# Combining four experts on one Trainium2 core: seven more result tiles loaded while the softmax ends, gates in seven parts instead of six, and the carry of maxima moved ahead of the last block's sums

## The reference, cut to what matters

```python
def gnn(features, edge_src, edge_dst, edge_weight, W, b):        # 12500 nodes, 200000 edges, 256 features
    msgs = features[edge_src] * edge_weight[:, None]
    agg = segment_sum(msgs, edge_dst)
    return agg @ W.T + b

def ffn(x):                                                      # M = 8192: edge_index names nodes 0..8191
    h = (x @ W_gat).reshape(M, 4, 4)                             # heads, experts
    src, dst = edge_index with a loop at every node              # 131072 edges
    e = leaky_relu((h * att_src).sum(-1)[src] + (h * att_dst).sum(-1)[dst], 0.2)
    alpha = softmax of e over the edges of each dst
    agg = segment_sum(h[src] * alpha[:, :, None], dst) + b_gat
    scores = (layernorm(agg) * gamma + beta).mean over heads     # one score for each expert
    g = softmax over the two best scores, 0 for the other two
    for ei in range(4):
        out += g[ei] * (gelu(x @ W1[ei] + b1[ei]) @ W2[ei] + b2[ei])

x = x + gnn(layernorm(x));  x = x + ffn(layernorm(x))
```

## Time and the profile before

| | us |
|---|---|
| median of three runs | 3670.58 |
| the profiled execution | 3668.62 |
| its span in the profile | 3666.8 |
| last expert pair's sum by DVE ends | 3449.2 |
| last block of the softmax can begin | 3462.12 |
| first gather of `combine` | 3488.62 |
| PE's first pair in `combine` | 3518.51 |
| PE's last sum copied out | 3663.65 |

### The profile page before, as it was taken

One profiled execution on the slowest core, in us unless ns is written; L12 is line 12 of the kernel. 1 busy time (PEld: TensorE's weight loads), 2 busy tenths in 40 slices (PEclk: granted clock), 3 DMA queues, 4 the chain that ended last, 5 costly groups with the idle time before them and its releaser, 6 DMA issues. The chain is left out here.

```text
span 3666.8 us, 60445 instructions
## 1 busy us (share of the span) xinstructions
PE 2973.6 (81%) x13893; PEld 2432.7 (66%) x13894; DVE 2042.9 (56%) x6851; ACT 817.8 (22%) x2321; POOL 2708.2 (74%) x2817
## 2 busy tenths in 40 slices
PE   1475665666866889978888799999999999999648
PEld 1354544554645666766666688888888888888537
DVE  8777778787787676664344223343343334242567
ACT  6300000000111111211222222223232322232247
POOL 6677777777777777777777777777777777777573
PEclk6786887887877999999999899999999999999879
DMA  9643333333433444444444222242223222322289
GB/s 347 198 120 106 107 111 111 112 114 112 116 115 111 121 122 124 128 119 127 128 128 131 58 73 54 54 122 54 73 54 76 54 74 53 79 73 54 57 299 366
DMA packets 276554, 424.71 MB, mean 116 GB/s; under 512 B 59704, under 2 KB 210211, under 8 KB 275363
## 3 DMA queue, kind: packets, MB, share of 16 engines
q0 software_dynamic: 114208, 216.64, 23.6%
q1 hardware_dynamic: 64175, 114.71, 8.6%
q10 hardware_dynamic: 98004, 91.50, 7.7%
HBM read 317.12 MB, written 105.97 MB: 115 GB/s over the span
## 5 line engine op out<-in xcount | busy, mean ns | idle before, releaser
L672 POOL DMA_INDIRECT rows<-feats,src_t x1500 | 1446.8, 965 | 466.9 <-issue 443.6
L1198 POOL DMA_INDIRECT got<-row_dram,src_sorted x1024 | 990.0, 967 | 312.1 <-issue 312.1
L833 PE MATMUL node_sums<-rows,ys_ahead 128*128 x3904 | 989.5, 408 | 231.6 <-SPq L656 101.2
L833 PEld LDWEIGHTS node_sums<-rows,ys_ahead 128*128 128x128 f32 x3904 | 762.4, 202 | 427.5 <-issue 314.9
L1282 PE MATMUL d_hidden<-d_yt,w 128*128 128x256 f32 x3136 | 711.9, 380 | 0.8 <-DVE d_yt L1368 0.8
L1293 PE MATMUL d_expert<-w,hid 128*128 128x256 f32 x3136 | 708.7, 379 | 0.0
L1293 PEld LDWEIGHTS d_expert<-w,hid 128*128 128x128 f32 x3136 | 596.7, 190 | 80.2
L1282 PEld LDWEIGHTS d_hidden<-d_yt,w 128*128 128x128 f32 x3136 | 595.0, 191 | 79.7 <-DVE d_yt L1368 1.2
L1345 DVE TENSOR_TENSOR yo<-d_expert,x_and_b 128x512 f32<-128x512 f32 x196 | 135.5, 691 | 837.5 <-PE d_expert L1293 829.9
L892 DVE TENSOR_SCALAR ys_ahead<-iota,rel,ew_t 128x128 f32<-128x128 f32 x1952 | 557.1, 364 | 65.3 <-DVE rel L888 2.3
L1226 ACT ACTIVATE hid<-d_hidden,b1c 128x256 f32<-128x256 f32 x784 | 323.7, 471 | 983.8 <-PE d_hidden L1282 792.7
(11 more groups left out here) (302 smaller groups left out, 2270.2 us busy)
## 6 DMA issues: line engine op xcount, KB each, us to landing
y_dram<-yo ACTq DMA_DIRECT2D x196, 256.0 KB, 2.2
ys<-y_dram SPq DMA_DIRECT2D x36, 1024.0 KB, 9.2
rows<-feats,src_t POOLq DMA_INDIRECT x1500, 2.8
got<-row_dram,src_sorted POOLq DMA_INDIRECT x1024, 2.4
ys_ahead<-y_dram SPq DMA_DIRECT2D x13, 1024.0 KB, 9.1
x_dram<-edge_plan ACTq DMA_DIRECT2D x98, 128.0 KB
d_x<-x_dram ACTq DMA_DIRECT2D x49, 256.0 KB, 3.1
ys_ahead<-in_x ACTq DMA_DIRECT2D x97, 128.0 KB
```

What stands on the lines that cost most here:

```text
L672: pool.indirect_dma_start(rows[:, g % RING, j, :], None, feats, bass.IndirectOffsetOnAxis(ap=m.src_t[:, g * GT + j:g * GT + j + 1], axis=0 ...
L833: t = pe.matmul(psA[:, ds(((code >> 1) & 1) * 512, FEAT)], hot[:, r, j, :], rows[:, ds((code >> 2) & (RING - 1), 1), j, :], start=False, s ...
L1198: pool.indirect_dma_start(got[:, k, j, 0:ROWF], None, m.row_dram, bass.IndirectOffsetOnAxis(ap=m.src_sorted[:, BEGIN[b] + j:BEGIN[b] + j + ...
```

## The change

It has these parts.

- `AHEAD` becomes 5: the early load takes in pair 4, whose buffer is now part of the tile `m.plan`. `SLOTS` becomes 17.
- `LATE` = 7: after the store of the seventh block's states, and once PE, DVE and the stores are through with all pairs, SP loads pairs 5 to 11. Their buffers are the tiles of the expert weights `w1` and `w2` and the tiles `hid`, `yo` and `x_and_b2`, which live on to the end of the program for that. In `combine` SP first loads the three small vectors, then pairs 12 to 16.
- `PART` has seven parts of 6, 12, 18, 20, 18, 16 and 8 tiles instead of six of 10, 18, 20, 20, 20 and 10. DVE sums every third pair of a part instead of every fourth (18 pairs instead of 17, PE 31 instead of 32).
- In the last block of the softmax DVE's 4 and 20 scans are issued without a wait between them.
- `carry` is split. `carry_across` of the maxima (turn, copy, scan) stands right behind the last block's `maxima`; `carry_back` stands behind its `sums`.
- Nodes without edges get a place of their own behind the edges (128 rows of zeros in `state_dram`, written once by SP). The bounds checks of `spread` and of the gather go, and so does POOL's clearing of `m.ns`. `positions` on DVE has three more small instructions.

```diff
-SLOTS = 16
-AHEAD = 4
+SLOTS = 17
+AHEAD = 5
+LATE = 7
...
     pool.indirect_dma_start(m.adst_first, bass.IndirectOffsetOnAxis(ap=m.first_pos[:, t:t + 1], axis=0),
-                            m.node_dst[:, t, :], None, bounds_check=GEDGES - 1, oob_is_err=False
-                            ).then_inc(m.s_sc, 16)
+                            m.node_dst[:, t, :], None).then_inc(m.s_sc, 16)
...
                     for k in range(AHEAD):
-                        load_pair(sp, m, k, k, m.ys_ahead[:, k])
+                        load_pair(sp, m, k, k, m.y_slots[k])
+                if b == len(BLOCK_PAIR) - 1:
+                    sp.wait_ge(s_l2, PAIRS * EXPERTS)
+                    sp.wait_ge(s_yo, PAIRS * EXPERTS)
+                    for e in range(EXPERTS):
+                        sp.wait_ge(s_st[e], 16 * PAIRS)
+                    for k in range(AHEAD, AHEAD + LATE):
+                        load_pair(sp, m, k, k, m.y_slots[k])
...
-            pool.memset(m.ns, 0.0).then_inc(s_clear, 1)
...
                 for ch in range(start, stop):
-                    c.done(v.tensor_tensor_scan(rows[:, :, ch], decay[:, head[ch], 0:n], rows[:, :, ch],
-                                                last[:, ch:ch + 1], ALU.mult, ALU.add))
+                    c.inc(v.tensor_tensor_scan(rows[:, :, ch], decay[:, head[ch], 0:n], rows[:, :, ch],
+                                               last[:, ch:ch + 1], ALU.mult, ALU.add))
+                    if b < BLOCKS - 1 or ch == stop - 1:
+                        v.wait_ge(s_v, c.n)
...
-            for b in range(len(BLOCK_PAIR), BLOCKS):
-                maxima(b)
-                messages(b)
-                sums(b, 0, ROWF)
-                block_end(b)
-
-            c.inc(v.tensor_copy(tail[:, 0, 0:HEADS], mx[:, :, 0]))
+            maxima(BLOCKS - 1)
+            c.inc(v.tensor_copy(tail[:, 0, 0:HEADS], mx[:, :, size(BLOCKS - 1)]))
...
-            carry(0, HEADS, -BIG, ALU.min, ALU.max)
+            carry_across(0, HEADS, -BIG, ALU.min, ALU.max)
+            messages(BLOCKS - 1)
+            sums(BLOCKS - 1, 0, ROWF)
+            block_end(BLOCKS - 1)
+            carry_back(0, HEADS)
...
-        PART = [0, 10, 28, 48, 68, 88, T]
+        PART = [0, 6, 18, 36, 56, 74, 90, T]
         PARTS = len(PART) - 1
         BY_VECTOR = [i for n in range(PARTS) for i in range(PART[n] // 2, PART[n + 1] // 2)
-                     if (i - PART[n] // 2) % (4 if n < PARTS - 1 else 2) == 0]
+                     if (i - PART[n] // 2) % (3 if n < PARTS - 1 else 2) == 0]
...
-            for k in range(AHEAD, SLOTS // 2):
-                load_pair(sp, m, k, k, y_of(k))
             for n, a in enumerate((b_gat, gamma, beta)):
                 sp.dma_start(vec[:, n, :], a.rearrange("(o c) -> o c", o=1).to_broadcast([P, HE])).then_inc(s_c, 16)
-            for k in range(SLOTS // 2, SLOTS):
+            for k in range(AHEAD + LATE, SLOTS):
                 load_pair(sp, m, k, k, y_of(k))
...
-                                            bass.IndirectOffsetOnAxis(ap=m.last_pos[:, t:t + 1], axis=0),
-                                            bounds_check=GEDGES - 1, oob_is_err=False).then_inc(s_got[part], 16)
+                                            bass.IndirectOffsetOnAxis(ap=m.last_pos[:, t:t + 1], axis=0)
+                                            ).then_inc(s_got[part], 16)
```

More of the change, by code:

```diff
@@ L98, in build @@
     m.adst_dram = dram("adst_dram", (NPAD, HEADS))
-    m.adst_first = dram("adst_first", (GEDGES, HEADS))
-    m.state_dram = dram("state_dram", (GEDGES, STATE))
+    m.adst_first = dram("adst_first", (GEDGES + NPAD, HEADS))
+    m.state_dram = dram("state_dram", (GEDGES + P, STATE))
     with ExitStack() as top:
@@ L128, in build @@
         m.s_store = [sem(f"tile_stored{k}") for k in range(SLOTS)]
-        layers = top.enter_context(ExitStack())
-        def weights(name, shape):
-            return layers.enter_context(nc.sbuf_tensor(name, shape, F32))
         m.plan = keep("edge_plan", [P, 3 * ECOLS])
         m.ns = m.plan[:, 0:TILES * STATE].rearrange("p (t c) -> p t c", c=STATE)
-        m.ys_ahead = keep("ys_ahead", [P, AHEAD, 2, EXPERTS, FEAT])
-        m.w1 = weights("w1", [P, HALVES, EXPERTS, HID])
-        m.w2 = weights("w2", [P, FB, EXPERTS, FEAT])
-        m.b1c = weights("b1c", [P, EXPERTS, FB])
-        m.b2r = weights("b2r", [P, EXPERTS, FEAT])
+        m.ys_ahead = keep("ys_ahead", [P, AHEAD - 1, 2, EXPERTS, FEAT])
+        m.w1 = keep("w1", [P, HALVES, EXPERTS, HID])
+        m.w2 = keep("w2", [P, FB, EXPERTS, FEAT])
+        m.b1c = keep("b1c", [P, EXPERTS, FB])
+        m.b2r = keep("b2r", [P, EXPERTS, FEAT])
         with ExitStack() as part1:
@@ L162, in build, with pairs_of @@
             weighted_sums(nc, sem, feats, edge_index, x, W, b, W_gat, att_src, att_dst, W1, b1, W2, b2, m)
+        m.hid = keep("hid", [P, 2, FB, N2])
+        m.yo = keep("yo", [P, EXPERTS, 2, FEAT])
+        m.xb = keep("x_and_b2", [P, EXPERTS, 2, FEAT])
+        def pairs_of(flat):
+            n = 2 * EXPERTS * FEAT
+            return [flat[:, a:a + n].rearrange("p (t e f) -> p t e f", e=EXPERTS, f=FEAT)
+                    for a in range(0, flat.shape[1] - n + 1, n)]
+        m.y_slots = [m.ys_ahead[:, k] for k in range(AHEAD - 1)] + pairs_of(m.plan[:, TILES * STATE:])
+        for t in (m.w1, m.w2, m.hid, m.yo, m.xb):
+            m.y_slots += pairs_of(t[:].rearrange("p a b c -> p (a b c)"))
+        assert len(m.y_slots) == AHEAD + LATE
         attention_and_experts(nc, sem, m)
-        layers.close()
         combine(nc, sem, b_gat, gamma, beta, out, m)
@@ L551, in weighted_sums @@
         tot = lent(TILES)
+        spare = lent(TILES)
         pos = lent(2 * TILES).rearrange("p (n t) -> p n t", n=2)
@@ L606, in weighted_sums @@
                     cur = 1 if cur == 2 else 1 - cur
-        PC = 13
+        PC = 14
         @block.sync
@@ L690, in _ @@
             c.inc(pool.memset(zeros[:], 0.0))
+            c.inc(pool.iota(spare[:], pattern=[[P, TILES]], base=GEDGES, channel_multiplier=1,
+                            allow_small_or_imprecise_dtypes=True))
             pool.wait_ge(s_pc, c.n)
@@ L703, in _ @@
             pool.wait_ge(s_pos, 1)
-            pool.wait_ge(s_zo, 16 * 8)
+            pool.wait_ge(s_zo, 16 * 9)
             pool.wait_ge(s_row, 1)
@@ L1025, in positions @@
                 c.done(v.tensor_tensor(pos[:, 1, :], pos[:, 0, :], cnt[:], ALU.add))
[L1027 to L1029 removed]
+                c.inc(v.tensor_tensor(pos[:, 0, :], pos[:, 0, :], spare[:], ALU.subtract))
+                c.done(v.tensor_scalar(pos[:, 1, :], pos[:, 1, :], 1.0, spare[:, 0:1], ALU.subtract, ALU.subtract))
+                c.inc(v.tensor_tensor(pos[:, 0, :], pos[:, 0, :], m.has_edges[:], ALU.mult))
+                c.done(v.tensor_tensor(pos[:, 1, :], pos[:, 1, :], m.has_edges[:], ALU.mult))
+                c.inc(v.tensor_tensor(m.first_pos[:], pos[:, 0, :], spare[:], ALU.add))
+                c.done(v.tensor_scalar(m.last_pos[:], pos[:, 1, :], spare[:, 0:1], None, ALU.add))
                 v.sem_inc(s_pos, 1)
@@ L1455, in pair, with carry_across @@
                         slot(i, e)
-            def carry(n, w, start, op0, op1):
+            def carry_across(n, w, start, op0, op1):
                 v.sem_inc(s_ask, 1)
@@ L1465, in carry, with carry_back @@
                 v.sem_inc(s_ask, 1)
+            def carry_back(n, w):
                 v.wait_ge(s_t, 2 * n + 2)
@@ L1506, in _ @@
             c.done(v.tensor_copy(tail[:, 1, HE:ROWF], factor[:, 1, :]))
-            carry(1, ROWF, 0.0, ALU.mult, ALU.add)
+            carry_across(1, ROWF, 0.0, ALU.mult, ALU.add)
+            carry_back(1, ROWF)
             v.wait_ge(s_row, 16)
```

40 lines of the change are left out of this document (17 added, 23 removed).

## The result

The changed kernel took 3675.32 us (median of 20 runs, 3672.78 to 3681.1), the kernel before 3669.81 us (20 runs on the same chip). The ratio is 1.0014, 95% interval 1.0008 to 1.002: slower by 5.5 us, clear of the scatter but within the 0.2% at which the prediction drew its line. The profiled execution's span is 3673.4 us, 6.6 more than before.

What follows compares the result with a forecast made beforehand. The prediction took a chain of DVE, ACT and PE to bound `combine`, with no DMA of expert outputs. `combine` beginning 1.2 us earlier and taking 7.1 longer gave 3670.58 + 5.9 = 3676.5 us, range 3664 to 3685.

Steps and rivals of the forecast that it cites:

- the working: `combine` scheduled by hand, part by part: 183.9 us for the new split, 176.8 for the old, so 7.1 us longer.
- What POOL is spared: Softmax's end: no clearing (2.09 us) and no bounds checks (2.5 us) bring the last edge gather 4.7 us earlier.
- The queue of loads: Softmax's end: seven early loads slow the last gather to 5.8 us and hold the eighth block's store until 3478.8.
- the loads don't hinder: Softmax's end, a rival: early loads delay nothing, `combine` begins 8.0 us earlier, total 3669.7 us; chance 8%.
- Unchaining and the carry: Last softmax block: 22 fewer waits save 2.7 us, the carry ahead costs 0.4 there; the gain is lost in the queue.
- `combine`'s parts: Seven parts start PE 6.8 us sooner but add a gates round and two long PE gaps: 7.1 us longer.
- DVE and ACT did not keep step: The faster rival for `combine` was that they do keep step: 10 us off, total 3659.3 us; chance 12%.
- the gap that should have been under 4 us: PE's gap before part 3 in `combine`: under 4 us would decide for the faster rival; the forecast had some 11.
- The lower clock behind short stops: Slower rival in `combine`: PE drops to the lower clock two or three times more, total 3681.7 us; chance 35%.
- stops of 2 to 3 us one pair apart: PE's stops in `combine` that the slower, lower-clock rival was said to need; that rival's chance 35%.
- DMA was no bound: The rival was that DMA bounds `combine`: eight loads less save 20.9 us, total 3649; chance 2%, counted with faster.

Runs made afterwards that it cites:

- f3: Changed kernel with the six parts of before and the seven late loads moved into `combine`; ratio to the kernel before 1.0002.
- e3: Changed kernel with the seven late loads issued behind the store of the eighth block's states instead of ahead of it; ratio to the kernel before 1.0023.
- e4: Changed kernel with a wait behind each of the last block's 24 scans again; ratio to the kernel before 1.0031.
- h1: Changed kernel, seven parts, with DVE waiting for the gathers of all tiles before the first part's gates; ratio to the kernel before 1.0075.
- h2: Changed kernel with the six parts of before and DVE waiting for all tiles' gathers before the first part's gates; ratio to the kernel before 1.0059.
- e1: Changed kernel with the gates in the six parts of before and every fourth pair on DVE; ratio to the kernel before 1.002.
- f1: Second run of the changed kernel with the six parts of before and every fourth pair on DVE; ratio to the kernel before 1.0021.
- g1: Changed kernel again, unaltered, on a chip where the kernel before took 6073 to 6139 us; ratio to the kernel before 1.0036.
- e2: Changed kernel with the seven late loads moved from the softmax's end to the start of `combine`, seven parts kept; ratio to the kernel before 1.001.
- f2: Second run of the changed kernel with the seven late loads moved into `combine`, seven parts kept; ratio to the kernel before 1.0018.

## Why the prediction was right, step by step

The total was within 1.2 us: 3676.5 forecast, 3675.32 measured. That it was so near is in part luck: `combine` began 2.5 us later than forecast, and it grew by 1.8 us less.

| step | forecast | measured |
|---|---|---|
| last edge gather issued | 3455.0 | 3458.11 |
| DVE begins the last block | 3460.8 | 3464.47 |
| from there to the last scan's end | 11.6 | 11.8 |
| row can be read | 3479.6 | 3482.08 |
| first gather of `combine` | 3487.4 (-1.2) | 3489.92 (+1.3) |
| PE's first pair behind it | 23.4 | 23.3 |
| first gather to the end | 183.9 (+7.1 by the working) | 183.5 (+5.3) |

- **What POOL is spared.** Mis-sized: 4.7 us forecast, 1.6 measured at the last edge gather. The clearing's 2.09 us went. The 98 `spread` operations gave 1.1 us from the first to the last and not 2.5 (median 958 ns against 972). And the kernel stood 1.26 us later already at the first `spread` (2029.53 against 2028.27); I took nothing for it and had no row for it, and no run shows where it comes from.
- **The queue of loads.** Right in kind: DVE could use the gather after 6.4 us (5.8 forecast), and the store landed 4.8 us behind its issue. Its end was mis-sized, and this, not POOL's part, is what turned -1.2 into +1.3, since the store waits for the queue: loads and store were forecast to be through by 3478.8, the store landed at 3481.4, and the row was read 2.5 us later than forecast. About 0.9 us of it is the later start (the seventh block's store was issued at 3454.14, not 3453.26), and, by an estimate, about 1 us comes from the stretch from 3458 to 3460, in which the full engines moved 215 GB/s and not 413; why isn't shown. f3 and e3 show that it is the loads that delay the store and POOL's small transfers.
- **The bound of "the loads don't hinder".** It had 8.0 us. With f3's stretch of 23.3 us behind a gather that lands in 2.4, `combine` would have begun at 3483.8, 4.8 us sooner than before (an estimate: 3458.11 + 2.4 + 23.3); 3.1 us of the difference is what POOL wasn't spared.
- **Unchaining and the carry.** Right: the 22 waits less are 2.89 us (2.7 forecast), and they are lost in the queue, on e4's chip in full, on that of the timing by the estimate above all but 0.8. The Trainium skill (VectorE: DVE Perf Modes, The DRAIN you can't avoid) says that leaving out semaphores saves nothing; here 20 scans took 4.77 us instead of 7.22, so the measurement decides against it. The carry ahead cost 0.8 us inside the block (14.98 us to the store in e4 against 14.22 before) and gave back 1.0 behind it (11.5 us from the last scan's end to the first gather in f3, 12.57 before): next to nothing.
- **`combine`'s parts.** Right in mechanism. DVE waited 4.96 and 3.17 us for the Exp of parts 2 and 3 (about 4 forecast), PE's gaps were 9.5 and 10.84 us (9 and 11). That the cost is the split's own is shown by h1 and h2, and by e1 and f1. Gates stood at 20.6, 39.7, 66.1, 93.7, 121.4, 146.3 and 168.7 us behind the first gather (forecast 20.8, 39.0, 65.7, 93.4, 121.6, 146.5, 168.8). The end came at 183.5 against 183.9. What was mis-sized is the difference: the working gave before 176.8 where 178.2 was measured, and its miss of 1.4 us went into the +7.1. Taking the working's 183.9 against the measured 178.2 would have given +5.7.
- **The rivals.** DVE and ACT did not keep step; the gap that should have been under 4 us was 10.84. The lower clock behind short stops did not come more often in the profiled execution, but once (four pairs behind a stop of 2.10 us took 15.74 us, where four behind one of 0.42 had taken 14.05; granted clock 0.53 in their first 3.5 us) instead of twice. That was near luck: g1, the same kernel with the same stops to 0.1 us, has it three times (15.74, 19.24 and 19.19 us). Nor do stops of 2 to 3 us one pair apart decide it: behind 1.93 and 2.06 us, one pair apart, it stayed away in the changed kernel and came in g1; before it also came behind a stop of 2.30 us with one of 1.16 ahead (seven pairs in 26.17 us, granted clock 0.60 in their first 3.4). The loads did hinder (f3). DMA was no bound: `combine` loads eight pairs fewer than before and got longer, with no load in the chain that ended last; and moved back into it, the loads did not lengthen it on the other chips (e2, f2).

## What to carry to other kernels

A transfer that nobody waits for is only free if nothing short and urgent shares its DMA engines: here seven early loads took back all that shorter scans and a lighter POOL had gained, both in front of a 528 KB store in their own queue and beside small transfers of another queue. A finer split starts the pipeline sooner but adds a round of its fixed steps; it pays only if each part still leaves the last engine enough work to cover the next round, so count that cover for the smallest parts first. Where two versions are compared by a hand-made schedule, set the new schedule against the measured old one too, and keep both differences in the range.

## What the runs showed of the hardware

- On two other chips the kernel before took 6073 to 6139 us (medians of four sets of runs) instead of 3670. In stretches beside POOL's indirect DMAs, issued 1.25 us apart as ever, DVE started dependent small operations 1.40 us apart instead of 0.25, and PE stood still for up to 37.7 us (g1). With POOL quiet DVE's last block took the same 11.80 us to the last scan's end, and PE's late stops were the same to 0.1 us; its pairs were not, where the clock differed. Why is open: the first part's gates ran beside gathers at full pace (g1), and in h1 the slow starts went on for up to 11 us behind the last gather.
- A store of 528 KB behind seven loads was readable 15.2 us after its issue (g1), without them 3.4 us (f3), with them behind it 3.8 us (e3); an indirect gather of one row for each partition, on another queue, took 5.3 us to its use beside them (e3) instead of 2.4 (g1).
